# ScalarE's PSUM scaling after the convolution replaced by a bias added to the input tile, with the scale moved into VectorE's add

## The chip, the cores and the metric

The kernel runs on one core of a Trainium2 chip. The metric is the device time in microseconds (us) of one launch; the times given are medians over several executions.

## What is computed

The input `x` has the shape (2, 8, 256, 256), float32. Four residual layers follow each other: an MLP, a 3x3 convolution, and two more MLPs. Each works on a group norm `_gn` of its input with four groups of two channels.

```python
def _L1_conv_ref(x, weight, bias):
    w = binarize(weight)          # sign(w) times the mean of |w| over each output channel
    xp = jnp.pad(x, ((0, 0), (0, 0), (1, 1), (1, 1)), mode='edge')
    out = lax.conv_general_dilated(xp, w, window_strides=(1, 1), padding='VALID', ...)
    return out + bias[None, :, None, None]

x = x + _L0_conv_ref(_gn(x), ...)     # per expert e: gelu(x @ w1 + b1) @ w2 + b2
x = x + _L1_conv_ref(_gn(x), L1_conv_weight, L1_conv_bias)
x = x + _L2_conv_ref(_gn(x), ...)
x = x + _L3_conv_ref(_gn(x), ...)
```

So the convolution's layer is `x + m * (signs convolved with gn(x)) + bias`, where `m` and the bias belong to the output channel.

## The kernel before, in words

Every engine has its own instruction stream in program order; semaphores join the streams. An MLP takes the eight channels (experts `E` counts them over the layers, 0 to 23) one after another: TensorE computes the first product (`g1`, line 1031) and the second (`g2`, lines 1049 to 1054), with every float32 operand split in a high part, which ScalarE rounds off (lines 561, 568, 578), and a low part, which VectorE subtracts (lines 714, 729, 735). The activations lie transposed in `XT`.

The convolution works on 20 tiles `q`: 10 for batch 0, then 10 for batch 1. A tile is two blocks of 16 image rows of all 8 channels on the 128 partitions, 256 columns each (the tenth tile of a batch holds one block). The blocks lie in the SBUF tensor `XC`, with one more column on either side. For each tile:

- GpSimd (`normalise_tile`, line 514) writes the normalised tile `CN`; it may run once `clo` of the tile two before is there, since `CN` has two buffers.
- ScalarE (line 632) rounds it to `Ch`, VectorE (`conv_low`, line 909) subtracts to get `Cl`.
- TensorE (line 1137) does six matmuls with the banded sign matrix `BAND` into one of four PSUM banks `ROT` (named `ACC` in the profile), and signals `conv_mm`.
- ScalarE (line 637) scales that bank in place by `conv_mean` and adds `conv_bias`, and signals `cscaled`.
- VectorE (`conv_add`, line 918) adds the bank to the tile in `XC`, and signals `cadded`.
- SyncE stores the tile to a DRAM scratch (line 455). After tiles 5, 7 and 9 of a batch, `read_x2` waits for the stores that it needs and reads groups of blocks back, transposed, into `XT` (line 445; two such calls after tile 9). SyncE does all this in one order: batch 0's stores and reads, then batch 1's.

The order on VectorE is written out: `conv_low(q)`, then `conv_add(q - 2)`, with the end of the last expert and the statistics of channel pair 3 of batch 1 put between them. After tile 16's low part VectorE waits for all of batch 0 to be back in `XT`:

```python
q = B * TILES
conv_low(q - 3)
dve.wait_ge(x2_in[0], 16 * len(pieces_back()))
sums(9, 0)
```

Then come the statistics of batch 0's first channel pair, the norm `XN` (line 724), its parts `Xh` (line 568) and `Xl` (line 729), and between them the last five adds. The next MLP (`pair(4, 1)`) begins with batch 0; batch 1 comes in when it has been stored, read back, and its statistics (job 10, lines 668, 675, 1010) made. Job 10's matmul stands in TensorE's own order, at the third step of expert 9's batch 0, so TensorE stops there until that job is ready.

Of the kernel before, what the change touches and what calls it, by code (L numbers as in the profile page):

```python
# [26 lines left out]
ALU = mybir.AluOpType  # L27
ACT = mybir.ActivationFunctionType
AX = mybir.AxisListType

B, C, N, D, H = 2, 8, 256, 256, 1024
# [14 lines left out]
NBLK = -(-D // OUTR)  # L46
# [3 lines left out]
TILES = -(-NBLK // 2)  # L50
CRING = 3
# [41 lines left out]
def slots(E, layer=None):  # L93

    return HT * (E + sum(E > h for h in HALVED)) if isinstance(E, int) else (
        HT * E + (len(HALVED) * HT if layer else 0))
# [118 lines left out]
def build(nc, x, w1, b1, w2, b2, cw, cb, out):  # L215
# [4 lines left out]
    with ExitStack() as ctx:  # L220
        def sb(name, shape, dt=F32, where=ctx):
            return where.enter_context(nc.sbuf_tensor(name, shape, dt))
# [4 lines left out]
        def sem(name):  # L227
            return ctx.enter_context(nc.semaphore(name))
# [32 lines left out]
        conv_bias = sb("conv_bias", [PART, 1])  # L261
        conv_mean = sb("conv_mean", [PART, 1])
# [10 lines left out]
        CN = sb("CN", [PART, 2, 2, NP])  # L273
# [7 lines left out]
        XC = sb("XC", [PART, B, NBLK, NP])  # L281
# [3 lines left out]
        with ExitStack() as use:  # L285
            Ch = sb("Ch", [PART, CRING, 2, NP], F32R, use)
# [9 lines left out]
        ROT = [ACC[1][0], ACC[1][1], ACC[0][0], ACC[0][1]]  # L296
# [18 lines left out]
        x1_last = [sem(f"x1_last{b}") for b in range(B)]  # L315
        xc_last = [sem(f"xc_last{b}") for b in range(B)]
        cst_done, pads = sem("cst_done"), sem("pads")
        cn_done, chi, clo, conv_mm, cscaled, cadded = (sem("cn_done"), sem("chi"), sem("clo"), sem("conv_mm"),
                                                       sem("cscaled"), sem("cadded"))
        x2_out = [[sem(f"x2_out{b}_{n}") for n in range(len(STORED))] for b in range(B)]  # L320
        x2_in = [sem(f"x2_in{b}") for b in range(B)]
        out_tr, out_evac = sem("out_tr"), sem("out_evac")
# [4 lines left out]
        def wait(eng, s, value):  # L327

            if not isinstance(value, int) or value > 0:
                eng.wait_ge(s, value)  # L330
# [205 lines left out]
        def _(act):  # L536
# [26 lines left out]
            def x_hi(E, par, b, layer):  # L563

                wait(act, xn_done, norm_of(E, b) + 1)

                wait(act, g1_done, slots(E - 1, layer) if known(E) != C + 2 else slot_of(C, (b + 1) * HT - 1) + 1)
                nc.scalar.activation(Xh[:, par, :, b], XN[:, b], ACT.Copy).then_inc(xhi, 1)
# [55 lines left out]

            act.wait_ge(prep, 5 + KS)
            act.wait_ge(g2_done, slots(C))
            for q in range(B * TILES + 2):
                if q < B * TILES:
                    w = 1 if q % TILES == TILES - 1 else 2
                    wait(act, cn_done, q + 1)  # L630
                    wait(act, conv_mm, q - CRING + 1)
                    nc.scalar.activation(Ch[:, q % CRING, 0:w], CN[:, q % 2, 0:w], ACT.Copy).then_inc(chi, 1)
                if q >= 2:
                    w = N if (q - 2) % TILES == TILES - 1 else 2 * N
                    wait(act, conv_mm, q - 1)
                    bank_q = ROT[(q - 2) % 4][:, 0:w]
                    nc.scalar.activation(bank_q, bank_q, ACT.Identity, bias=conv_bias[:, 0:1],
                                         scale=conv_mean[:, 0:1]).then_inc(cscaled, 1)
            x_hi(C, 0, 0, 1)
            for k in range(4):  # L640
                w_hi(C + 1, 1, k, 1)
# [14 lines left out]
        def _(dve):  # L656
# [215 lines left out]
            for i in range(4):  # L872
                e, b = divmod(i, B)
# [38 lines left out]
            def conv_add(q):  # L912
                b, i = divmod(q, TILES)
                own = slice(2 * i, min(2 * i + 2, NBLK))
                w = own.stop - own.start
                wait(dve, cscaled, q + 1)
                at = XC[:, b, own, 1:N + 1]
                nc.vector.tensor_tensor(at, ROT[q % 4][:, 0:w * N].rearrange("p (k n) -> p k n", k=w),  # L918
                                        at, ALU.add).then_inc(cadded, 1)

            for q in range(B * TILES - 3):
                conv_low(q)
                if q >= 2:
                    conv_add(q - 2)
                if q == 1:
                    evict(C - 1, 1, C - 1, 0, 1)
                if q == 2:
                    dve.wait_ge(evicted, evicts(C))
                    sums(8, C - 2)
                if q == 3:  # L930
                    sums_done(8)
                    aggregate(8)
                if q == 4:
                    deviate(8)
                if q == 6:
                    add_eps(8)
                if q == 7:
                    scale_shift(8, NPAIR - 1)
                    dve.wait_ge(st_done, 9)
                    to_partitions(1)  # L940
                    double_edges(1)

            q = B * TILES
# [3 lines left out]
            sums_done(9)  # L947
            aggregate(9)
            conv_add(q - 5)
            conv_low(q - 2)  # L950
            deviate(9)
            conv_add(q - 4)
            add_eps(9)
            conv_low(q - 1)
# [223 lines left out]
```

## Time and profile before

| | |
|---|---|
| median of 3 runs | 631.81 us (631.55 to 632.73) |
| profiled execution, first to last instruction (its span) | 629.2 us |
| its own time with what lies around the span | not given apart; the median is 2.6 us above the span |
| TensorE busy | 596.4 us (95%) |
| ScalarE busy | 430.6 us (68%) |
| VectorE busy | 423.5 us (67%) |
| mean granted TensorE clock | 0.981 |

All times in the rows are microseconds from the first instruction, unless marked ns. TensorE is PE (its weight loads PEld), VectorE DVE, ScalarE ACT, GpSimd POOL, and SPq the DMA queue that SyncE issues on. The duration of an instruction overlaps the next one's on the same engine: the distance between two starts is shorter than the duration. The releaser of a wait is inferred from the semaphores. The convolution lies between 202 and 251 us.

### The profile page before, as it was taken

The numbers are of one execution on the slowest core, as the hardware profiler recorded it, in microseconds if no ns is written. First come the engines' busy times: TensorE is split into PE (matmuls) and PEld (weight loads), VectorE is DVE, ScalarE is ACT, GpSimd is POOL, SyncE is SP. The second block draws the span as 40 slices with busy tenths as digits, with TensorE's granted clock in tenths as the row PEclk, the third lists the DMA queues.
The fourth block names the chain that finished last, engine by engine and source line by source line (L and its number), as shares of the span: only waits on it lengthen the run. The fifth ranks groups of instructions, "written<-read, shape, count | busy, mean of one in ns | idle before, by whom it ended". The sixth has DMA issues, their size and how long they took to land.

```text
span 629.2 us, 9514 instructions
## 1 busy us (share of the span) xinstructions
PE 596.4 (95%) x2973; PEld 503.7 (80%) x2973; DVE 423.5 (67%) x857; ACT 430.6 (68%) x741; POOL 31.4 (5%) x52
## 2 busy tenths in 40 slices
PE   8999999999999974959999999999999999999997
PEld 7778888888898753859988888888888888888885
DVE  4777967866795965546876767856855865765632
ACT  5767667767776762726977767767776767777753
POOL 2000000000001540000000000000000000000000
PEclk9999999999999996979999999999999999999999
DMA  8762464445545654630423232231423424334001
GB/s 269 201 213 100 141 174 141 128 145 148 184 121 165 202 180 160 185 71 2 134 67 135 67 111 91 72 129 67 133 68 102 150 85 132 118 86 152 30 18 67
DMA packets 57500, 77.78 MB, mean 124 GB/s; under 512 B 3942, under 2 KB 50806, under 8 KB 56950
## 3 DMA queue, kind: packets, MB, share of 16 engines
q1 hardware_dynamic: 57462, 77.31, 39.1%
q8 instruction: 19, 0.31, 0.2%
q14 instruction: 19, 0.16, 0.1%
HBM read 63.90 MB, written 13.40 MB: 123 GB/s over the span
## 4 chain that ended last, share of the span: by engine, by line
PE 82%; DMA 8%; DVE 5%; issue 2%; POOL 1%; ACT 1%; SPq 1%; DVEq 0%; POOLq 0%; ACTq 0%
PE G L1031 40%; PE ACC L1054 13%; PE ACC L1049 13%; PE ACC L1050 13%; DMA XT<-x_scratch 3%; DMA x_scratch<-XC 3%; DMA W2raw<-in_L_conv_w 1%; DVE Cl L909 1%; DVE XC L918 1%; DVE BN L668 1%; PE TR L1067 1%; DMA W1raw<-in_L_conv_w 1%; PE TR L997 1%; PE STAT L1010 0%; SPq L445 0%
## 5 line engine op out<-in xcount | busy, mean ns | idle before, releaser
L735 DVE TENSOR_TENSOR Hl<-HR,Hh 128x512 fp32r<-128x512 f32 (+1 forms) x216 | 136.2, 630 | 160.0 <-ACT Hh L578 158.6
L574 ACT ACTIVATE HR<-G,BT 128x512 f32<-128x512 f32 (+1 forms) x216 | 138.5, 641 | 146.7 <-PE G L1031 145.5
L1031 PE MATMUL G<-Xh,W1l 128*128 128x512 f32 (+1 forms) x432 | 164.2, 380 | 3.4 <-issue 2.0
L1031 PE MATMUL G<-Xl,W1h 128*128 128x512 f32 (+1 forms) x432 | 159.1, 368 | 0.0
L1031 PE MATMUL G<-Xh,W1h 128*128 128x512 f32 (+1 forms) x432 | 159.0, 368 | 0.0
L1049 PE MATMUL ACC<-Hh,W2l 128*128 128x512 f32 (+1 forms) x432 | 156.7, 367 | 0.0
L1050 PE MATMUL ACC<-Hh,W2h 128*128 128x512 f32 (+1 forms) x432 | 156.4, 367 | 0.0
L578 ACT ACTIVATE Hh<-HR 128x512 fp32r<-128x512 f32 (+1 forms) x216 | 126.3, 585 | 8.7
L1054 PE MATMUL ACC<-Hl,W2h 128*128 128x512 f32 (+1 forms) x432 | 123.4, 367 | 0.3 <-DVE Hl L735 0.3
L1031 PEld LDWEIGHTS G<-Xh,W1l 128*128 128x128 f32 x432 | 82.5, 191 | 15.6 <-issue 2.2
L1031 PEld LDWEIGHTS G<-Xh,W1h 128*128 128x128 f32 x432 | 82.3, 191 | 13.5
L1049 PEld LDWEIGHTS ACC<-Hh,W2l 128*128 128x128 f32 x432 | 82.1, 190 | 13.4
L1050 PEld LDWEIGHTS ACC<-Hh,W2h 128*128 128x128 f32 x432 | 82.1, 190 | 13.2
L1031 PEld LDWEIGHTS G<-Xl,W1h 128*128 128x128 f32 x432 | 82.6, 191 | 11.5
L1054 PEld LDWEIGHTS ACC<-Hl,W2h 128*128 128x128 f32 x432 | 78.2, 189 | 14.1 <-DVE Hl L735 0.9
L714 DVE TENSOR_TENSOR W2l<-W2raw,W2h 128x512 fp32r<-128x512 f32 x96 | 65.6, 685 | 3.6 <-ACT W2h L561 2.9
L714 DVE TENSOR_TENSOR W1l<-W1raw,W1h 128x512 fp32r<-128x512 f32 x96 | 65.5, 685 | 1.7 <-ACT W1h L561 1.4
L561 ACT ACTIVATE W2h<-W2raw 128x512 fp32r<-128x512 f32 x96 | 58.8, 615 | 3.0 <-DMA W2raw<-in_L_conv_w 3.0
L561 ACT ACTIVATE W1h<-W1raw 128x512 fp32r<-128x512 f32 x96 | 58.6, 616 | 1.1 <-DMA W1raw<-in_L_conv_w 1.1
L668 DVE BATCH_NORM_STATS2 BN<-XT 128x6 f32<-128x512 f32 (+1 forms) x60 | 37.3, 680 | 19.5 <-DMA XT<-x_scratch 19.5
L508 POOL TENSOR_TENSOR RS<-VE,half 128x2 f32<-128x2 f32 (+1 forms) x18 | 12.8, 710 | 506.2 <-DVE VE L692 506.2
L729 DVE TENSOR_TENSOR Xl<-XN,Xh 128x512 fp32r<-128x512 f32 x48 | 32.9, 685 | 0.3
(73 smaller groups left out, 359.6 us busy)
## 6 DMA issues: line engine op xcount, KB each, us to landing
W1raw<-in_L_conv_w SPq DMA_DIRECT2D x24, 1024.0 KB, 5.0
W2raw<-in_L_conv_w SPq DMA_DIRECT2D x24, 1024.0 KB, 5.6
x_scratch<-XC SPq DMA_DIRECT2D x18, 256.0 KB, 2.8
x_scratch<-XT SPq DMA_DIRECT2D x16, 256.0 KB
out_x<-OUTT SPq DMA_DIRECT2D x16, 256.0 KB, 2.2
XC<-x_scratch SPq DMA_DIRECT2D x16, 252.0 KB
NAT<-in_x SPq DMA_DIRECT2D x6, 512.0 KB, 8.4
XT<-x_scratch SPq DMA_DIRECT2D x4, 672.0 KB
```

What stands on the lines that cost most here:

```text
L508: nc.gpsimd.tensor_tensor(RS[:, bs], VE[:, bs], half[:, bs], ALU.pow).then_inc(rs_done, 1)
L561: nc.scalar.activation(dst, src, ACT.Copy).then_inc(whi, 1)
L574: nc.scalar.activation(HR[:, t % 2, 0:n], G1[t % 2][:, 0:n], func, bias=BT[:, bass.ds(col, 1)]).then_inc(gelu_done, 1)
L578: nc.scalar.activation(Hh[:, t % RING, 0:n], HR[:, t % 2, 0:n], ACT.Copy).then_inc(hhi, 1)
L668: nc.vector.bn_stats(BN[:, b, i], at).then_inc(bn_done, 1)
L714: nc.vector.tensor_tensor(dst, src, high.bitcast(F32), ALU.subtract).then_inc(wlo, 1)
L729: nc.vector.tensor_tensor(Xl[:, par, :, b], XN[:, b], Xh[:, par, :, b].bitcast(F32), ALU.subtract).then_inc(xlo, 1)
L735: nc.vector.tensor_tensor(Hl[:, t % RING, 0:n], HR[:, t % 2, 0:n], Hh[:, t % RING, 0:n].bitcast(F32), ALU.subtract).then_inc(hlo, 1)
L1031: ins = nc.tensor.matmul(G1[t % 2][:, 0:width(b)], w[:, ee, c, col], rhs, start=n == 0, stop=n == len(parts) - 1)
L1049: nc.tensor.matmul(banks[m][:, 0:n], W2l[:, ee, t8, col], high, start=t8 == 0, stop=False)
L1050: nc.tensor.matmul(banks[m][:, 0:n], W2h[:, ee, t8, col], high, start=False, stop=False)
L1054: ins = nc.tensor.matmul(banks[m][:, 0:n], W2h[:, ee, t8, col], Hl[:, t % RING, 0:n], start=False, stop=t8 == HT - 1)
```

## The change

ScalarE no longer touches PSUM in the convolution. Behind each `Ch` it adds `conv_bias` to the tile of `XC` in place, which GpSimd has read by then, and signals `cbiased`. VectorE waits for `cbiased` and directly for the matmuls (`conv_mm`), and computes `bank * conv_mean + XC` in one scalar_tensor_tensor.

```diff
-            for q in range(B * TILES + 2):
-                if q < B * TILES:
-                    w = 1 if q % TILES == TILES - 1 else 2
-                    wait(act, cn_done, q + 1)
-                    wait(act, conv_mm, q - CRING + 1)
-                    nc.scalar.activation(Ch[:, q % CRING, 0:w], CN[:, q % 2, 0:w], ACT.Copy).then_inc(chi, 1)
-                if q >= 2:
-                    w = N if (q - 2) % TILES == TILES - 1 else 2 * N
-                    wait(act, conv_mm, q - 1)
-                    bank_q = ROT[(q - 2) % 4][:, 0:w]
-                    nc.scalar.activation(bank_q, bank_q, ACT.Identity, bias=conv_bias[:, 0:1],
-                                         scale=conv_mean[:, 0:1]).then_inc(cscaled, 1)
+            for q in range(B * TILES):
+                b, i = divmod(q, TILES)
+                own = slice(2 * i, min(2 * i + 2, NBLK))
+                w = own.stop - own.start
+                wait(act, cn_done, q + 1)
+                wait(act, conv_mm, q - CRING + 1)
+                nc.scalar.activation(Ch[:, q % CRING, 0:w], CN[:, q % 2, 0:w], ACT.Copy).then_inc(chi, 1)
+                at = XC[:, b, own, 1:N + 1]
+                nc.scalar.activation(at, at, ACT.Identity, bias=conv_bias[:, 0:1]).then_inc(cbiased, 1)
...
-                wait(dve, cscaled, q + 1)
+                wait(dve, cbiased, q + 1)
+                wait(dve, conv_mm, q + 1)
                 at = XC[:, b, own, 1:N + 1]
-                nc.vector.tensor_tensor(at, ROT[q % 4][:, 0:w * N].rearrange("p (k n) -> p k n", k=w),
-                                        at, ALU.add).then_inc(cadded, 1)
+                nc.vector.scalar_tensor_tensor(at, ROT[q % 4][:, 0:w * N].rearrange("p (k n) -> p k n", k=w),
+                                               conv_mean[:, 0:1], at, ALU.mult, ALU.add).then_inc(cadded, 1)
```

On ScalarE the order at the start of the convolution, before:

```order
L632 ACTIVATE Ch<-CN 128x516 [waits cn_done,g2_done,prep]
L632 ACTIVATE Ch<-CN 128x516 [waits cn_done] x2
L637 ACTIVATE ACC_0<-ACC_0,conv_bias,conv_mean 128x512 [waits conv_mm]
L632 ACTIVATE Ch<-CN 128x516 [waits conv_mm,cn_done]
L637 ACTIVATE ACC_1<-ACC_1,conv_bias,conv_mean 128x512 [waits conv_mm]
```

and with the change:

```order
L633 ACTIVATE Ch<-CN 128x516 [waits cn_done,g2_done,prep]
L635 ACTIVATE XC<-XC,conv_bias 128x2x256
L633 ACTIVATE Ch<-CN 128x516 [waits cn_done]
L635 ACTIVATE XC<-XC,conv_bias 128x2x256
L633 ACTIVATE Ch<-CN 128x516 [waits cn_done]
```

There were three `Ch` before the first other activation; now each tile's bias stands directly behind its `Ch`, tiles 0 and 1 included.

## Rows read from the trace of the kernel before

**Rows 1.** The page: busy time and share of each engine.
```profile
PE 596.4 (95%) x2973; PEld 503.7 (80%) x2973; DVE 423.5 (67%) x857; ACT 430.6 (68%) x741; POOL 31.4 (5%) x52
```
**Rows 2.** Windows: stretch, its length, engines' busy time, PE clock, DMA share, GB/s.
```profile
203.00:222.40 19.40, 17.36 (x75) 12.92 (x76) 17.91 (x38) 14.17 (x24) 10.77 (x15) 1.00 0.67 218
232.30:241.40 9.10, 0.00 (x0) 0.00 (x0) 0.00 (x0) 0.01 (x1) 0.00 (x0) 0.56 0.54 192
280.00:629.00 349.00, 344.70 (x1670) 289.55 (x1669) 226.92 (x433) 248.26 (x421) 5.39 (x8) 1.00 0.28 91
```
**Rows 3.** Chain that ended last, in order of time: start, length, engine, tile, line.
```profile
222.36 9.88 DMA x_scratch<-XC
...
241.43 1.30 DVE BN L668 x2
...
251.50 7.37 DMA x_scratch<-XC
...
259.57 12.73 DMA XT<-x_scratch
272.32 1.30 DVE BN L668 x2
```
**Rows 4.** Groups of whole trace by shape: busy us, mean ns, idle before.
```profile
L918 DVE TENSOR_TENSOR XC<-ACC,XC 128x512 f32<-128x512 f32 x18 | 12.2, 680 | 0.0
L749 DVE SCALAR_TENSOR_TENSOR XT<-ACC,BT,XT 128x512 f32<-128x512 f32 x18 | 12.6, 740 | 0.0
L637 ACT ACTIVATE ACC<-ACC,conv_bias,conv_mean 128x512 f32<-128x512 f32 x18 | 13.3, 738 | 14.1 <-PE ACC L1137 14.1
L574 ACT ACTIVATE HR<-G,BT 128x512 f32<-128x512 f32 x168 | 115.9, 690 | 121.5 <-PE G L1031 120.9 <-DVE Hl L735 0.4
L578 ACT ACTIVATE Hh<-HR 128x512 fp32r<-128x512 f32 x168 | 106.3, 633 | 7.2
```
**Rows 5.** Timeline of VectorE and GpSimd, two full periods, tiles 8 to 12.
```profile
219.09 0.68 DVE L918 TENSOR_TENSOR XC<-ACC,XC 128x512 f32<-128x512 f32 x1
219.26 0.78 POOL L514 TENSOR_SCALAR CN<-XC,CST 128x516 f32<-128x516 f32 x1 [0.37 <-DVE Cl L909]
219.69 0.89 DVE L909 TENSOR_TENSOR Cl<-CN,Ch 128x516 fp32r<-128x516 f32 x1
220.68 0.77 POOL L514 TENSOR_SCALAR CN<-XC,CST 128x516 f32<-128x516 f32 x1 [0.64 <-DVE Cl L909]
221.10 0.89 DVE L909 TENSOR_TENSOR Cl<-CN,Ch 128x516 fp32r<-128x516 f32 x1
```
**Rows 6.** Timeline of the start: ScalarE, VectorE, GpSimd, tiles 0 to 2.
```profile
203.14 1.31 ACT L632 ACTIVATE Ch<-CN 128x516 fp32r<-128x516 f32 x2 [1.72 <-POOL CN L514]
204.48 0.70 DVE L909 TENSOR_TENSOR Cl<-CN,Ch 128x516 fp32r<-128x516 f32 x1
204.60 1.22 POOL L514 TENSOR_SCALAR CN<-XC,CST 128x516 f32<-128x516 f32 x1 [0.82 <-DVE Cl L909]
205.10 0.87 DVE L749 SCALAR_TENSOR_TENSOR XT<-ACC,BT,XT 128x256 f32<-128x256 f32 x2
206.53 0.70 DVE L909 TENSOR_TENSOR Cl<-CN,Ch 128x516 fp32r<-128x516 f32 x1 [0.56 <-ACT Ch L632]
```
**Rows 7.** Timeline around the join with the next MLP, DVE and ACT.
```profile
247.81 0.55 DVE L724 TENSOR_SCALAR XN<-XT,ST 128x512 f32<-128x512 f32 x1
248.28 0.69 DVE L918 TENSOR_TENSOR XC<-ACC,XC 128x512 f32<-128x512 f32 x1
248.39 0.63 ACT L568 ACTIVATE Xh<-XN 128x512 fp32r<-128x512 f32 x1
249.06 0.69 DVE L729 TENSOR_TENSOR Xl<-XN,Xh 128x512 fp32r<-128x512 f32 x1
```
**Rows 8.** Chain after TensorE's second stall: one matmul of 256 columns each.
```profile
275.98 0.21 PE ACC L1049
...
278.53 0.12 PE ACC L1049
```

More of the change, by code:

```diff
@@ L317, in build @@
         cst_done, pads = sem("cst_done"), sem("pads")
-        cn_done, chi, clo, conv_mm, cscaled, cadded = (sem("cn_done"), sem("chi"), sem("clo"), sem("conv_mm"),
-                                                       sem("cscaled"), sem("cadded"))
+        cn_done, chi, clo, conv_mm, cbiased, cadded = (sem("cn_done"), sem("chi"), sem("clo"), sem("conv_mm"),
+                                                       sem("cbiased"), sem("cadded"))
         x2_out = [[sem(f"x2_out{b}_{n}") for n in range(len(STORED))] for b in range(B)]
```

## The prediction

> **What bounds the kernel now.** I read the page's busy times first. TensorE works 596.4 of 629.2 us, VectorE and ScalarE some 425 each [rows 1]. That is an average over two different regimes, so the windows come next. After 280 us TensorE is busy for 344.7 of 349 us and runs at the full clock [rows 2]: whatever delay or gain reaches that point passes to the end one for one, and nothing later is touched by this change. In the convolution (203 to 222.4 us) VectorE is busy 17.91 of 19.40 us, more than TensorE's 17.36 or ScalarE's 14.17; then all compute engines stand still from 232.3 to 241.4 us [rows 2].
>
> The chain of waits says why. It runs through VectorE's adds and low parts to the add of tile 9, which ends at 222.36 us; the store of that tile is issued then and lands 9.88 us later, the read back follows, and only then come the statistics of 241.43 us. Batch 1 repeats this: its last store takes 7.37 us, its last reads 12.73, and the statistics at 272.32 let TensorE go on [rows 3]. So only two instants matter: when tile 9's add ends , and when the last store of batch 1 is issued (251.50). ScalarE is not in this chain at all. The decisive reading is in the groups: before the 18 large adds VectorE was idle for 0.0 us [rows 4]. They never waited for ScalarE's scaling, so taking it out of their way gives them nothing.
>
> **The change, part by part.**
>
> *Removed: 20 scalings of PSUM.* ScalarE loses 18 x 738 ns and two shorter ones. Their only large wait, 14.1 us for TensorE [rows 4], lies in the standstill. Value on the chain: 0. At the join the last scaling stood before `Xh`, but `Xh` starts at 248.39, where `XN` (247.81 + 0.55 = 248.36) has just become ready [rows 7]: at most 0.03 us.
>
> *Added: 20 bias adds, SBUF to SBUF, with one pointer operand.* The trace has no such instruction. Below lies the copy without a pointer, 633 ns; above, the scaling with two pointers, 738; I take the activation with one bias pointer, 690 [rows 4]. ScalarE has the time: per tile 0.63 + 0.69 us overlapped, against a period of 1.41 us (219.69 to 221.10) [rows 5]. The bias of tile q is done about two periods before the add of tile q asks for it.
>
> The exception is the start. `Ch` of tiles 0 and 1 now run back to back from 203.14 us [rows 6]; with a bias between them the second starts at about 204.28 (0.54 behind the first, plus 0.60 for the bias) and ends at 204.92. Its low part, begun at 204.48 in the trace, then comes at 204.95, after GpSimd's `CN` of tile 2 has begun at 204.60. In the trace that `CN` took 1.22 us instead of 0.78 because the low part ran first; now GpSimd goes first, is done at 205.38, and the low part ends some 0.53 us behind it, at 205.91. (The 0.53 is from the steady rows: `CN` ends at 220.04 and 221.45, the low parts at 220.58 and 221.99 [rows 5].) The two evictions behind it move from 205.10 to 205.82, end their turn 0.79 later, and the next low part starts at 206.61 instead of 206.53 [rows 6], since 0.56 us of idle time was there to be used. Cost: 0.08 us.
>
> *Changed: the add.* It becomes a scalar_tensor_tensor with one PSUM tensor, one pointer and one SBUF tensor. This shape is in the trace: the eviction at line 749, 740 ns against 680 ns for the present add [rows 4]. The difference is 0.06 us per tile. It isn't paid ten times. In the steady period the low part lasts 0.89 us instead of 0.70 [rows 5, 6], because it ends 0.54 us behind GpSimd's `CN`, whenever it began; an add that is 0.06 longer only shortens that stall of 0.2. The Trainium skill (SBUF — State Buffer, Who interferes with whom) says the same as a rule: a VectorE instruction with two SBUF inputs and a GpSimd one that reads SBUF exclude each other for the whole instruction. Of the adds of batch 0, five (tiles 1, 3, 6, 7, 8) are followed by such a stalled low part, and tile 5's by a wait for GpSimd's square root. Exposed are tiles 0, 2, 4 and 9: 4 x 0.06 = 0.24 us. With the start, tile 9's add ends 0.32 us later.
>
> *The second instant.* Before the read of batch 1's second group SyncE waits for the add of tile 17 (248.28 + 0.69 = 248.97 [rows 7]); +0.06 us there. For VectorE this one is free, since `Xl` waits for `Xh` until 249.06 [rows 7]. The adds of 18 and 19 lie behind SyncE's own issuing. Cost: 0.06 us.
>
> *Wait added.* The add now waits for `conv_mm` itself; that comes earlier than `cscaled` did, so nothing is queued longer.
>
> **The sum.** 0.08 + 0.24 + 0.06 = +0.38 us if the transfers pass all of the first delay on. From below: 0.06 if tile 9's store, which takes 9.88 us because earlier transfers are in front of it, lands when it did. From above: all ten adds exposed, 0.60 + 0.08 + 0.18 = 0.86. I take +0.4, being nearest to a chain with one transfer behind another. The profiled execution's span is 629.2 us and would be 629.6; its own total is not shown, the median of 631.81 lies 2.6 above the span, and I keep that difference: **632.2 us**. A change under 0.2% (1.26 us) can't be told from none: the three runs themselves span 1.18 us.
>
> **The rivals.**
>
> *Slower: the new add shuts GpSimd out.* It has a pointer in SBUF besides the SBUF tensor. If the pair counts as two SBUF inputs, `CN` waits for the end of the add, and the low part for the end of `CN`. An add starts before `CN` (219.09 against 219.26 [rows 5]), so this decides from the first tile on. The period becomes 0.58 (rest of the add) + 0.78 + 0.54 = 1.90 us instead of 1.41; over the eight tiles 2 to 9 that is 3.9 us, hence about 636 us. Against it: the two evictions of the same kind at 205.10 to 205.97 took 0.87 us, while `CN` ran beside them and ended at 205.82 [rows 6]; locked out it would have begun at 205.97. Chance 4%. The Trainium skill, same section, lets a VectorE instruction with at most one SBUF input pass; it doesn't say how a pointer counts, and the trace decides for passing.
>
> *Slower or faster: the clock after the second stall.* After the statistics of 272.32 a matmul of 256 columns takes 0.21 us on the chain, and from 278.53 on 0.12 [rows 8]: some 3.3 us of matmuls at 1.2 instead of 2.4 GHz, on the path. If the slow stretch falls twice as long or is missing, with the restart moved by a few tenths, 15 matmuls x 0.09 = 1.4 us are lost or won: 633.6 or 630.8. The trace has one case only and can't say. Chance 6% each way.
>
> *Slower or faster: the transfers.* One store takes 9.88 us and another 7.37 [rows 3]; shifted by tenths against the traffic in front of them, the reads may land a microsecond or more earlier or later, 630.5 to 634. Chance 4% slower, 3% faster.
>
> *The change gives what it takes away.* If adds had waited for the scaling, up to 0.7 us a tile would come back, several us in all, 627. The 0.0 us of idle time speaks against it; 1%.
>
> **How the numbers follow.** The forecast has the remaining 76%; it lies well within the bound of 0.2%. Slower: 4 + 6 + 4 = 14%; faster: 6 + 3 + 1 = 10%. The range of 80% takes the sum's own bounds (631.9 to 632.7), the spread of medians (half a microsecond each way), and the nearer half of the clock and transfer cases: 630.9 to 633.6.
>
> **What would show it.** Right: the new add at about 740 ns; idle before it still 0.0; low parts in the steady period shorter, about 0.83 us, at a period that stays at 1.41; the bias at 0.69 us; tile 9's add ending near 222.7 and the statistics of batches 0 and 1 at 241.7 and 272.7. Wrong: `CN` starting only as the add ends; adds that wait for `cbiased`; an add of 680 ns or less; a first statistics instruction unmoved, or moved by far more than tile 9's add.

## The result, and the profile after

| | before | changed |
|---|---|---|
| median | 632.12 us (18 runs) | 633.95 us (18 runs) |
| ratio to before | 1 | 1.0027, 95% interval 1.0016 to 1.0038 |
| span of the profiled execution | 629.2 us | 632.7 us |

The change makes the kernel slower by 0.27%, some 1.7 us. Of all the executions behind the ratios here and below one is left out, of e13, with 2094.62 us. The forecast was 632.2 in a range of 630.9 to 633.6, most likely no measurable change. Every execution takes some 2.0 us more than its span (634.73 for 632.7 in the profiled one after), so the profiled execution before, with its span of 629.2, was a short one of its kind, about 0.9 us under the median; that after is a long one, and a second profile of the same kernel (below) has a span of 632.1. Of the 3.5 us between the two spans 0.4 lie ahead of the convolution's first low part, 2.3 between it and the statistics of batch 1, and 0.8 behind these.

First the instructions that the sum priced. Groups of the whole trace after, by shape (busy us, mean ns, idle before), as [rows 4]:

```profile
L906 DVE TENSOR_TENSOR Cl<-CN,Ch 128x516 fp32r<-128x516 f32 x18 | 14.3, 792 | 2.2 <-ACT Ch L633 2.2
L916 DVE SCALAR_TENSOR_TENSOR XC<-ACC,conv_mean,XC 128x512 f32<-128x512 f32 x18 | 13.3, 740 | 0.0
L635 ACT ACTIVATE XC<-XC,conv_bias 128x512 f32<-128x512 f32 x18 | 12.8, 709 | 0.0
```

The new add takes 740 ns, as priced, and still never waits. The bias takes 709 ns, where 690 was taken. The steady period, VectorE and GpSimd, as [rows 5]:

```profile
219.94 0.77 POOL L514 TENSOR_SCALAR CN<-XC,CST 128x516 f32<-128x516 f32 x1 [0.38 <-DVE Cl L906]
220.42 0.83 DVE L906 TENSOR_TENSOR Cl<-CN,Ch 128x516 fp32r<-128x516 f32 x1
221.17 0.74 DVE L916 SCALAR_TENSOR_TENSOR XC<-ACC,conv_mean,XC 128x512 f32<-128x512 f32 x1
221.35 0.77 POOL L514 TENSOR_SCALAR CN<-XC,CST 128x516 f32<-128x516 f32 x1 [0.64 <-DVE Cl L906]
221.83 0.83 DVE L906 TENSOR_TENSOR Cl<-CN,Ch 128x516 fp32r<-128x516 f32 x1
```

The low part has become 0.06 us shorter (0.83 for 0.89), the period is 1.41 us as before, and `CN` starts beside the add and not behind it: GpSimd isn't shut out. All that is as forecast. Now the start, as [rows 6], in the timeline of ScalarE, VectorE and GpSimd:

```profile
203.56 0.63 ACT L633 ACTIVATE Ch<-CN 128x516 fp32r<-128x516 f32 x1 [1.72 <-POOL CN L514]
204.10 0.71 ACT L635 ACTIVATE XC<-XC,conv_bias 128x512 f32<-128x512 f32 x1
204.71 0.62 ACT L633 ACTIVATE Ch<-CN 128x516 fp32r<-128x516 f32 x1
...
205.02 0.77 POOL L514 TENSOR_SCALAR CN<-XC,CST 128x516 f32<-128x516 f32 x1 [0.82 <-DVE Cl L906]
...
204.23 0.70 DVE L906 TENSOR_TENSOR Cl<-CN,Ch 128x516 fp32r<-128x516 f32 x1 [1.75 <-ACT Ch L633]
205.37 0.97 DVE L906 TENSOR_TENSOR Cl<-CN,Ch 128x516 fp32r<-128x516 f32 x1 [0.44 <-ACT Ch L633]
206.26 0.87 DVE L746 SCALAR_TENSOR_TENSOR XT<-ACC,BT,XT 128x256 f32<-128x256 f32 x2
207.05 0.71 DVE L906 TENSOR_TENSOR Cl<-CN,Ch 128x516 fp32r<-128x516 f32 x1
```

This execution was 0.42 us late already when the first low part began (204.23 for 203.81), before anything had changed, so everything below is counted from that first low part. The evictions begin 2.03 us behind it instead of 1.29, a delay of 0.74 where 0.72 was worked out, and the third low part is 0.10 later where 0.08 was. But somebody waits for the evictions. SyncE's queue before and after; the first row of each is the store of expert 7's batch 1, the last the first reload of `XC` from it:

```profile
205.99 0.37 SPq L397 DMA_DIRECT2D x_scratch<-XT  x1
206.40 0.33 SPq L399 DMA_DIRECT2D x_scratch<-XT  x1
206.78 0.26 SPq L400 DMA_DIRECT2D x_scratch<-XT  x1
208.35 0.88 SPq L412 DMA_DIRECT2D XC<-x_scratch  x1
```

```profile
207.15 0.37 SPq L397 DMA_DIRECT2D x_scratch<-XT  x1
207.56 0.33 SPq L399 DMA_DIRECT2D x_scratch<-XT  x1
207.93 0.26 SPq L400 DMA_DIRECT2D x_scratch<-XT  x1
211.30 0.88 SPq L412 DMA_DIRECT2D XC<-x_scratch  x1
```

The store is issued 0.74 us later, as the evictions are. The reload, which waits for it to land, loses another 1.79 us: it begins 4.15 us behind the store's issue and not 2.36. Behind the reload, in SyncE's one order, stand all stores of tiles and all reads back. The chain of the changed kernel, as [rows 3] (start, length, what):

```profile
223.09 11.31 DMA x_scratch<-XC
...
243.54 1.30 DVE BN L665 x2
...
253.63 8.33 DMA x_scratch<-XC
...
262.66 12.32 DMA XT<-x_scratch
275.01 1.30 DVE BN L665 x2
```

Tile 9's store is issued 0.31 us later behind the first low part (18.86 for 18.55; forecast 0.32), but takes 11.31 us instead of 9.88. The statistics of batch 0 come 39.31 us behind the first low part, before it was 37.62: 1.69 us, of which tile 9's add accounts for 0.31.

### The profile page after: what moved, and what is told of

Same layout as the page of the kernel before. It is cut to its first block, busy times and chain, and to the rows that moved or that the text cites. A ratio compares the mean times of both kernels' runs of the same rounds, so it can differ in the third digit from the quotient of the medians.

```text
span 632.7 us, 9534 instructions
## 1 busy us (share of the span) xinstructions
PE 596.8 (94%) x2973; PEld 503.9 (80%) x2973; DVE 424.8 (67%) x857; ACT 429.7 (68%) x741; POOL 30.4 (5%) x52
## 4 chain that ended last, share of the span: by engine, by line
PE 82%; DMA 8%; DVE 4%; issue 2%; ACT 1%; POOL 1%; SPq 1%; DVEq 0%; POOLq 0%; ACTq 0%
PE G L1029 40%; PE ACC L1052 13%; PE ACC L1047 13%; PE ACC L1048 13%; DMA XT<-x_scratch 3%; DMA x_scratch<-XC 3%; DMA W2raw<-in_L_conv_w 1%; DVE BN L665 1%; DVE Cl L906 1%; PE TR L1065 1%; DMA W1raw<-in_L_conv_w 1%; DVE XC L916 1%; PE TR L995 1%; PE STAT L1008 0%; SPq L445 0%
## 5 line engine op out<-in xcount | busy, mean ns | idle before, releaser
L568 ACT ACTIVATE Xh<-XN 128x512 fp32r<-128x512 f32 x48 | 29.7, 620 | 20.9 <-DVE XN L721 20.8
```

## The experiments

Three theories. **Q**: the bias between the `Ch` of tiles 0 and 1 makes the evictions late, and these the store, the reload and SyncE's queue. **S**: the longer add is what costs. **K**: the slow-clock stretch behind the second stall is longer by chance. For each run the table has the ratio to before and, from its one profile, the stretches from the first low part in us: to the evictions, to the issue of the store of expert 7's batch 1, to the reload, to tile 0's store, to the statistics of batch 0, and to those of batch 1.

| run | ratio (95%) | evictions | store | reload | tile 0's store | statistics 0 | statistics 1 |
|---|---|---|---|---|---|---|---|
| before | 1 | 1.29 | 2.18 | 4.54 | 7.38 | 37.62 | 68.51 |
| changed | 1.0027 (1.0016 to 1.0038) | 2.03 | 2.92 | 7.07 | 9.91 | 39.31 | 70.78 |
| e16 changed again | 1.0021 (1.0003 to 1.0039) | 2.04 | 2.92 | 6.85 | 9.68 | 39.11 | 70.16 |
| e1 | 0.9994 (0.9977 to 1.0011) | 1.29 | 2.19 | 4.52 | 7.36 | 37.80 | 68.36 |
| e2 | 1.0024 (1.0012 to 1.0036) | 2.04 | 2.94 | 6.60 | 9.44 | 39.09 | 69.54 |
| e3 | 1.0009 (0.9996 to 1.0022) | 1.29 | 2.19 | 4.50 | 7.34 | 37.73 | 68.56 |
| e4 | 0.9998 (0.9985 to 1.0010) | -1.15 | -0.25 | 3.99 | 6.83 | 37.66 | 68.23 |
| e5 | 1.0004 (0.9987 to 1.0020) | -1.14 | -0.24 | 3.88 | 6.71 | 37.78 | 68.34 |
| e8 | 0.9996 (0.9984 to 1.0008) | -1.16 | -0.25 | 3.94 | 6.78 | 37.27 | 67.73 |
| e11 | 1.0014 (1.0003 to 1.0026) | 1.29 | 3.44 | 6.41 | 9.25 | 38.96 | 69.60 |
| e12 | 1.0012 (1.0000 to 1.0024) | 1.28 | 2.71 | 6.60 | 9.43 | 38.88 | 69.78 |
| e13 | 1.0031 (1.0007 to 1.0056) | 2.03 | 2.92 | 6.64 | 9.48 | 39.11 | 69.71 |
| e14 | 1.0038 (1.0018 to 1.0058) | 1.29 | 2.19 | 4.52 | 7.35 | 37.25 | 70.12 |
| e15 | 1.0019 (0.9998 to 1.0040) | -1.14 | -0.24 | 3.99 | 6.83 | 37.18 | 70.75 |
| e17 | 1.0021 (1.0004 to 1.0038) | 2.03 | 2.92 | 6.90 | 9.74 | 39.00 | 69.78 |
| e18 | 1.0027 (1.0013 to 1.0041) | 1.28 | 2.18 | 4.51 | 7.98 | 40.51 | 71.36 |

**e1: the changed kernel, each bias two tiles behind its `Ch`.**

```diff
-            for q in range(B * TILES):
...
+            for q in range(B * TILES + 2):
+                if q < B * TILES:
...
+                    nc.scalar.activation(Ch[:, q % CRING, 0:w], CN[:, q % 2, 0:w], ACT.Copy).then_inc(chi, 1)
+                if q >= 2:
+                    b, i = divmod(q - 2, TILES)
+                    at = XC[:, b, 2 * i:min(2 * i + 2, NBLK), 1:N + 1]
+                    nc.scalar.activation(at, at, ACT.Identity, bias=conv_bias[:, 0:1]).then_inc(cbiased, 1)
```

> The changed kernel with each bias add two tiles behind its Ch, where the scalings stood. Theory Q (the evictions: the bias between the Ch of tiles 0 and 1 makes tile 1's low part and the two evictions late, these hold the store of expert 7's batch 1 and, in SyncE's one queue, the reload of XC, all stores of tiles and all reads back): the evictions start about 1.3 us behind the first low part as before, SyncE's first tile store about 7.4 us behind it (9.9 in the changed kernel), and the time is within 0.1% of before, 632.1 to 632.7. Theory S (the add, 0.06 us longer each, is what costs): nothing moves but 0.1 us, ratio to before still 1.002 to 1.003. Theory K (the slow-clock stretch behind the second stall is longer by chance of its place): ratio anywhere from 0.998 to 1.003, and it follows the length of that stretch, not the store.

The ratio is 0.9994: the loss is gone, though the longer adds and all 20 bias adds are in place. Store, reload and first tile store stand where they stood before.

**e2: the kernel before, one activation more.**

```diff
+                    if q == 0:
+                        nc.scalar.activation(spare[:], spare[:], ACT.Identity, bias=conv_bias[:, 0:1])
```

> The kernel before with its adds and scalings untouched and one activation more on ScalarE, on a spare tile, between the Ch of tiles 0 and 1. It leaves the result as it is. Theory Q: the evictions come 0.7 us later, SyncE's first tile store 2 to 3 us later, ratio to before 1.002 to 1.0025 (633.4 to 633.7). Theory S: no add is longer, ratio 1.000 to 1.0003. Theory K: no statement on the sign, the time follows the slow stretch.

The instruction works on a spare tile that GpSimd clears once, at 3.1 us. One instruction of 0.71 us on an engine that isn't in the chain gives 1.0024, about all of the loss. ScalarE's timeline in e2, and SyncE's queue:

```profile
204.32 0.63 ACT L634 ACTIVATE Ch<-CN 128x516 fp32r<-128x516 f32 x1 [1.73 <-POOL CN L515]
204.86 0.71 ACT L636 ACTIVATE spare<-spare,conv_bias 128x512 f32<-128x512 f32 x1
205.47 0.62 ACT L634 ACTIVATE Ch<-CN 128x516 fp32r<-128x516 f32 x1
...
207.92 0.37 SPq L398 DMA_DIRECT2D x_scratch<-XT  x1
...
211.58 0.88 SPq L413 DMA_DIRECT2D XC<-x_scratch  x1
```

**e3: the kernel before with the longer add alone.** The edit is the change's tensor_tensor to scalar_tensor_tensor, with ScalarE left as it was. The convolution's term is then scaled twice and its bias once, so the kernel computes something else; nothing else is different.

> The kernel before, with ScalarE as it was (scaling and bias in PSUM, each bank) and only the add replaced by the scalar_tensor_tensor with the pointer conv_mean, so the convolution's term and its bias are scaled twice. Theory Q: the evictions and SyncE's first store stay, tile 9's add ends 0.24 us later, ratio 1.0003 to 1.0008. Theory S: ratio 1.002 to 1.003, all of the change's loss.

1.0009, and the interval contains 1. Tile 9's store is issued 0.40 us later (18.95), and the statistics of batch 0 come only 0.11 later. S explains at most a part: by the medians (632.67 for 631.97) 0.7 us, by the profile's two statistics 0.1.

**e4: the kernel before with the evictions first**, moved ahead of tile 0's low part.

```diff
+            evict(C - 1, 1, C - 1, 0, 1)
             for q in range(B * TILES - 3):
                 conv_low(q)
...
-                if q == 1:
-                    evict(C - 1, 1, C - 1, 0, 1)
```

> The kernel before with the two evictions of expert 7's batch 1 ahead of tile 0's low part instead of behind tile 1's; VectorE is idle there for 1.75 us. Theory Q: they end about 2.4 us earlier, SyncE stores and reloads that much earlier, as far as its transfers allow, and the tile stores are then held by the adds alone; 0.5 to 1.5 us faster than before, ratio 0.9975 to 0.9992. Theory S: 0.08 us at most, ratio 1.000. Theory K: no statement.

A miss for the gain that Q promised: the store is issued 2.4 us earlier, but its packets stand behind those of the weights, so that the reload comes only 0.55 earlier; and from tile 3 on SyncE waits for the adds, as it does in the kernel before. Earlier than before buys nothing.

**e5: the same edit in the changed kernel.**

> The changed kernel with the two evictions ahead of tile 0's low part; bias adds directly behind each Ch and the longer add stay. Theory Q: with the store of expert 7's batch 1 on its way before the low parts, the late low part of tile 1 holds nobody in SyncE's queue; first tile store about 7 us behind the first low part (9.9 in the changed kernel), ratio to before 1.000 to 1.001. Theory S: ratio stays 1.0025.

1.0004. The bias is still between the `Ch` of tiles 0 and 1, the low part of tile 1 is still late, and nobody in SyncE's queue waits for it any more.

**e11 and e12: the kernel before, SyncE made to wait alone.**

```diff
+                if b == 1:
+                    sp.wait_ge(clo, 3)
                 store_x1(C - 1, (b,), x1_last[b])
```

(e12 has `chi, 3`.)

> The kernel before with every compute engine as it was; only SyncE waits for tile 2's low part before it stores expert 7's batch 1, some 1.3 us later than before (3.5 us behind the first low part, where before is 2.2 and the changed kernel 2.9). Theory Q: that alone gives the changed kernel's loss or more, ratio 1.002 to 1.004, first tile store about 10 us behind the first low part. Theory S: 1.000. If the matter is the evictions' delay on VectorE and not SyncE's queue: 1.000.

> The same with the wait for tile 2's Ch, 0.5 us later than before (2.7 us). Theory Q with an edge (the store is late only when the 2 MB of weights in front of it have drained, 3 us behind the first low part): little or nothing, ratio 1.000 to 1.001, if still before the edge; 1.002 if behind it. Without an edge the first tile store comes 0.5 us later and the ratio is 1.0008.

No compute engine has another instruction or order, and the ratios are 1.0014 and 1.0012: SyncE's late start costs by itself, and the evictions' delay on VectorE isn't needed. That is less than Q expected of e11 (1.002 to 1.004). In the profiles both have nearly e2's delay at batch 0's statistics (1.34 and 1.26 us; e2 1.47), in the time half of its loss; the intervals overlap, e12's reaches down to 1.0000, and whether the other half is noise isn't settled. The two are alike although one store is issued 0.5 us behind its place in the kernel before (e12) and the other 1.3 (e11). Their reloads come at 6.60 and 6.41, both some 2 us late: it is an edge between 2.19 and 2.71 us, not a slope. SyncE's queue in e12, and the chain's row of tile 9's store:

```profile
206.78 0.37 SPq L397 DMA_DIRECT2D x_scratch<-XT  x1
207.19 0.33 SPq L399 DMA_DIRECT2D x_scratch<-XT  x1
207.56 0.26 SPq L400 DMA_DIRECT2D x_scratch<-XT  x1
210.67 0.88 SPq L412 DMA_DIRECT2D XC<-x_scratch  x1
...
222.60 11.23 DMA x_scratch<-XC
```

Tile 9's store is issued 18.53 us behind the first low part, as before (18.55), and takes 11.23 us instead of 9.88. This length has two levels over the runs. With the reload at 6.41 or later (changed, e16, e2, e11, e12, e13, e17) it is 11.14 to 11.35 us; with the reload at 4.54 or earlier 9.45 to 9.88 (before, e1, e3, e4, e5, e8). In e14, e15 and e18 other transfers stand in front of it.

**e16: the changed kernel again.**

> The changed kernel itself once more, for a second profile. Theory Q: the stretch from the first low part to batch 0's statistics is again 39.1 to 39.4 us (37.6 before), the stretch to batch 1's statistics and the slow-clock stretch behind it vary by half a microsecond, ratio 1.002 to 1.0035. Theory K: without the 6 us of slow clock of the first profile the ratio falls under 1.0015.

1.0021, with 39.11 us to batch 0's statistics. Windows behind the second stall (stretch, length, busy times, granted clock, DMA), of the changed kernel's first profile and of e16:

```profile
280.00:282.00 2.00, 2.00 (x10) 2.00 (x11) 0.09 (x1) 0.31 (x1) 0.00 (x0) 0.50 0.00 0
282.00:284.00 2.00, 2.00 (x15) 2.00 (x14) 0.70 (x4) 0.76 (x3) 0.54 (x1) 0.71 0.00 0
```

```profile
280.00:282.00 2.00, 2.00 (x17) 2.00 (x17) 0.42 (x1) 0.56 (x2) 0.00 (x0) 0.89 0.00 0
282.00:284.00 2.00, 2.00 (x19) 2.00 (x19) 0.93 (x5) 1.23 (x3) 0.54 (x1) 1.00 0.00 0
```

In the first profile TensorE started again at 276.59 and ran at 1.2 GHz until about 283 us; in e16 it started again at 276.95 and ran so until about 280.2. So K is real as a scatter: from batch 1's statistics to its norm the profiles take between 8.30 us (e3) and 9.05 (e1), and from these statistics to the end of the span 356.5 (e3) to 357.7 (changed), 356.9 in the kernel before, whatever the edit. It isn't what makes the difference. The delay stands ahead of batch 1's statistics, and e2's 12 runs have a mean granted clock of 0.9772 against 0.9766 of the kernel before beside them, and are slower all the same. (The ratio of e16 alone, from 1.0003 on, wouldn't exclude K.)

**e8, e14, e15: is there a faster version?** e8 is e5 with tile 9's add directly behind tile 8's:

```diff
-                if q >= 2:
+                if q >= 2 and q != 11:
                     conv_add(q - 2)
+                if q == 10:
+                    conv_add(9)
```

e14 is the kernel before, e15 is e8, each with the second group's read behind tile 9's store:

```diff
-GROUPS = [(6, 5), (10, 7), (16, 9), (NBLK, TILES - 1)]
+GROUPS = [(6, 5), (10, 9), (16, 9), (NBLK, TILES - 1)]
```

> The same, and the add of tile 9 directly behind that of tile 8, ahead of tile 11's low part. Only the changed kernel can have it that early: there the add waits for the matmuls and not for a scaling behind them. Theory Q: tile 9's store is issued about 0.8 us earlier; as the store lands behind earlier transfers half to all of it reaches the statistics, ratio to before 0.9985 to 1.000. If the landing is set by the transfers in front alone, the ratio is that of the kernel without the early add.

> The kernel before with the read back of the second group (384 KB) issued behind the store of tile 9 instead of behind that of tile 7, so that the last stores have less in front of them. If tile 9's store is held by the transfers in front of it, it lands 1 to 3 us sooner, and the statistics come earlier by what the later read doesn't take back: ratio 0.997 to 1.000. If the whole is held by the bytes to be moved, 1.000 to 1.002.

> The changed kernel with the evictions first, the add of tile 9 directly behind that of tile 8, and the second group's read behind tile 9's store. Tile 9's store can then be issued about 1.3 us earlier than before. Ratio 0.996 to 0.999 if the transfers in front hold that store; 0.9995 to 1.001 if the bytes do.

None is clearly faster than before. e8 has the earliest statistics of batch 1 (67.73) and 0.9996, not to be told from e1's 0.9994. Its early add, right behind tile 8's, is done by 17.5 us behind the first low part, but SyncE is busy issuing the second group's read until 17.9 and then stores tile 8, so that tile 9's store is issued at 18.42. In e14 tile 9's store, with 448 KB less issued in front of it (384 in the expectation), lands in 4.31 us. It does bring batch 0's statistics forward by 0.37 us, and loses 1.6 us by batch 1's, where the same edit puts the read later too: 1.0038. In e15 the same happens.

**e13, e17, e18: why an edge?** The 256 KB store follows 2 MB of weights. The guess was that it must be issued before those have drained. e13 puts a load of 288 KB in front of it, e17 two stores of 192 KB, both in the changed kernel (of e17's edit the wait for the tile that is stored isn't shown); e18, in the kernel before, moves 1 MB of the weights behind the reload.

```diff
+                    sp.dma_start(spare[:], w1[1][2, 0:PART, 0:576]).then_inc(extra, 16)
```

```diff
+                    for i in range(2):
+                        sp.dma_start(junk[i], diag[:].rearrange("p k c j -> p (k c j)")).then_inc(extra, 16)
```

```diff
                 if b == 0:
                     load_w1(1, 1, C + 1)
-                    load_w2(1, 1, C + 1)
+            load_w2(1, 1, C + 1)
```

> The changed kernel with one useless load of 288 KB behind the two loads of weights, so that the transfer engines are still busy when the late store of expert 7's batch 1 is issued. Theory Q with an edge: the store lands sooner although there is more to move, the reload begins at most 5.3 us behind the first low part (7.1 in the changed kernel), and the ratio to before falls from 1.0027 to 1.0005 to 1.0015. If it's only the amount of traffic or the lateness of the store itself: ratio 1.0027 or more.

> The changed kernel with two useless stores of 197 KB (a constant tile to a DRAM scratch) behind the loads of weights, so that these drain about 1.1 us later, 3.5 us behind the first low part; the late store of expert 7's batch 1 (2.9) is then again issued before the engines run dry, as in the kernel before (2.2 against 2.6). Theory Q with an edge at the drain: the block and its two rows land together, the reload begins about 5.5 us behind the first low part instead of 7, although more is moved; ratio 1.001 to 1.002. If lateness alone counts: reload at 7 or later, a slow tail of the rows again, ratio 1.0027 or more.

> The kernel before with the load of expert 9's second weights (1 MB) moved behind the reload of XC, so that the transfer engines run dry before the store of expert 7's batch 1 is issued, at the same time as before. Theory Q with an edge at the drain: with less in front of it the store lands later, the slow tail of the rows appears, reload 5.6 to 6.6 us behind the first low part (4.5 before). If lateness of the issue alone counts: reload at 4.5 or earlier. The time mixes this with the weights now in the way of the tiles, 1.001 to 1.004.

The guess fell, three times. With more in front the reload still begins at 6.64 and 6.90 (e13's addition had drained 0.2 us before the store's first packet, e17's hadn't); with 1 MB less it begins at 4.51, as before. So neither drained transfer engines nor their load makes the difference.

What does is in the packets. Windows in the kernel before, over the store's packets and behind them; the last two columns are the transfer engines' share and GB/s:

```profile
206.80:207.80 1.00, 1.00 (x6) 0.78 (x5) 1.00 (x3) 1.00 (x3) 0.47 (x1) 1.00 0.87 281
207.80:208.30 0.50, 0.50 (x4) 0.40 (x3) 0.50 (x2) 0.50 (x2) 0.30 (x1) 1.00 0.00 0
```

and in the changed kernel:

```profile
208.00:209.00 1.00, 1.00 (x6) 0.81 (x5) 1.00 (x3) 0.83 (x2) 0.63 (x1) 1.00 0.82 264
209.00:209.80 0.80, 0.57 (x3) 0.13 (x1) 0.80 (x3) 0.80 (x2) 0.00 (x0) 1.00 0.00 0
209.80:211.20 1.40, 0.94 (x5) 0.65 (x5) 1.40 (x4) 0.21 (x2) 0.77 (x1) 1.00 0.05 12
```

Nearly all of the block moves in 1 us in both. In the changed kernel 17 of its 276 packets, 16 of 1 KB and one of 4 bytes, come after a pause of 0.8 us, one by one, and the store counts as landed only with the last. 276 packets over 16 transfer engines are 17 for each, so this looks like the share of a single engine. The DMA view shows what that engine may have been doing. In the stretch 208.10 to 208.30 of the changed kernel (queue and kind, packets, MB, share of 16 engines):

```profile
q1 hardware_dynamic: 63, 0.06, 93.6%
q8 instruction: 1, 0.02, 51.8%
```

and in the kernel before, in the stretches 206.80 to 207.76 and 207.76 to 207.90:

```profile
q1 hardware_dynamic: 274, 0.26, 82.3%
q8 instruction: 1, 0.02, 55.8%
```

A single packet of 16 KB, of the kind that the profile calls "instruction" and on another queue, takes 1.66 us of one engine in the changed kernel (51.8% of 16 x 0.20 us) and 1.25 us in the kernel before. In the changed kernel it begins at 208.16 us, among the store's packets, and ends at 209.82; the store's late packets begin at 209.81. In the kernel before it begins at 207.77, when the last 1 KB packet of the store has begun. By the packets' times this holds for all 16 profiles: in the nine with the store issued at 2.19 or earlier the 16 KB packet doesn't begin before the store's last 1 KB packet, and in the seven others it begins among the store's packets or ahead of them, and the store's last packet ends 0.9 to 1.0 us behind the end of the 16 KB packet. It begins 3.8 to 4.1 us behind the first low part in those seven, and the store's packets begin some 0.9 us behind the issue and take as long again if nothing holds them: that is the edge. The trace doesn't say which engine a packet is on, and no run moves the 16 KB packet, so that it holds the store back is read from these times and not shown by an experiment.

## Why the prediction was wrong

- **Removed scalings worth 0**: right. The adds had no idle time and have none now, and no run shows a gain from it.
- **The add 0.06 us longer, paid at four tiles of ten**: right in the trace. It is 740 ns, and tile 9's store came 0.31 us later; the low parts became shorter by what the adds grew. e1, which keeps these adds, is at 0.9994 (up to 1.0011); e3 leaves room for 0 to 0.2% of loss, so their price in the total isn't settled, only small. By the profiles the statistics of batch 0 come 0.1 to 0.2 us later in both, less than the sum had.
- **GpSimd shut out**: no, as forecast. `CN` starts in the middle of the add, so the pointer doesn't count as a second SBUF input. The Trainium skill's rule (SBUF — State Buffer, Who interferes with whom) agrees with the low parts, which end 0.54 us behind `CN`.
- **The step that failed is "Cost: 0.08 us" at the start.** Its working was right to hundredths (evictions 0.74 us later, next low part 0.10) and it stopped on VectorE, because idle time there swallowed the delay. The evictions are also the work that SyncE waits for before it stores expert 7's batch 1, and behind that store stand the reload and every store and read of the tiles. A term for it was missing. By the runs it measures 1.3 to 1.5 us at batch 0's statistics (e12, e11, e2) and 0.12 to 0.24% of the time (e12, e2). Of the reload's delay of 2.53 us in the changed kernel 0.74 is the later issue; the other 1.79 come with the packets that stay behind.
- **"So only two instants matter"** was wrong with it: the chain named tile 9's add, but the store behind that add lands when the transfers in front of it have, and these hang on when SyncE begins. Before, SyncE caught up with the adds at tile 3; begun 2.5 us later, it catches up behind tile 5, and the first read back of 672 KB is issued 1.47 us later. Tile 9's store, issued at the forecast place, takes 1.43 us longer. The second instant, the last store of batch 1, comes 1.71 us later behind the first low part (49.40 for 47.69) and not 0.38.
- **The clock and the transfers** had 6% and 4% on the slow side. What lies behind batch 1's statistics scatters by up to 1.2 us, the clock's slow stretch with it, but not with the edits. The transfers are where the loss arose, though by SyncE's order and not by shifted tenths, and that deserved more than 4%.
- **The base** was the median of 3 runs, 631.81 us; over 18 runs it is 632.12. So 0.3 us of the 1.75 between forecast and result are not the change's. The 2.6 us between span and median are 2.0 in each execution; the rest was that the profiled one was short.

## What to carry to other kernels

When a step is moved on an engine, follow every consumer of everything that is queued behind it, the queue that issues DMAs among them; idle time on that engine says only that the engine itself loses nothing. A DMA-issuing engine with one fixed order turns one late wait into a late start of all that follows. Where a transfer lands late by a jump, look in the same stretch for packets of another queue, those of kind "instruction" among them. Here the helper instruction did no harm two tiles behind its `Ch`: e1 keeps the whole change and gives the loss back.

## What the runs showed of the hardware

- The landing of a store isn't smooth in its issue: 2.36 us from the issue to the following reload in the kernel before, 3.89 in e12 with the store issued 0.5 us later, 4.15 in the changed kernel, and again 2.97 in e11 with it still later. The extra is a pause and then 17 packets out of 276, which begin when a 16 KB packet of kind "instruction" ends; that packet took 1.0 to 1.7 us in the 16 profiles.
- A low part on VectorE (two SBUF inputs) ends 0.54 us behind a `CN` of GpSimd that began first, and `CN` runs 1.22 us instead of 0.78 when the low part began first; a scalar_tensor_tensor from PSUM, with a pointer and one tensor in SBUF, passes beside it.
- The stretch before the convolution varies too: the first low part begins between 203.8 and 205.2 us in kernels whose instructions up to there are the same on every compute engine.
